# Moving the normalisations in a two-layer window attention: q's norm into the exponentials, the division by the sums to the values' output, and the first maxima ahead of two loads

## The chip, the core and the metric

The kernel runs on one core of one Trainium2 chip. The metric is the device time of one execution in microseconds (us). The core has five engines that follow their own instruction streams and meet at semaphores: PE (TensorE: matrix multiplications and the transposes made with them), DVE (VectorE), ACT (ScalarE), POOL (GpSimd) and SP (SyncE), which here only issues DMA transfers.

## What is computed

The input x is 4 x 1024 x 128 in float32. First comes a latent attention of 16 heads with 8 columns each, between two layer norms. Then come two layers, each made of a window attention of 8 heads with 64 columns and an MLP, and a last norm and residual. The change lies in the way that the first attention's rows of maxima are sent, and in the window attention, of which this is the core:

```python
q = l2norm(q) * qs                      # l2norm(t) = t / clip(|t|, 1e-12), per head
k = l2norm(k) * ksc
q, k = rotary_xpos(q, k)                # q * cos * scale + rotate_half(q) * sin * scale, k with / scale
bq = q.reshape(b, h, w, 64, d) * 8.0    # windows of 64 rows, QK_SCALE
sim = einsum('bhwid,bhwjd->bhwij', bq, bk)     # keys of this window and of the one before
attn = softmax(where(mask, -max, sim))
out = einsum('bhwij,bhwjd->bhwid', attn, bv)
x = x + out @ wo
```

The norm of q is one number for each row and head. It can be applied to q, or to q's scores. The sum of a row's exponentials is one number for each row and head as well. It can divide the probabilities, or the row of the output.

## The kernel before, in words

The kernel is five functions in a row, each a block in which all engines have a stream of their own: `project`, `attend` (the first attention), `mix`, then `window` and `mlp` twice, then `last_norm`.

In `project`, SP writes the bf16 parts of q and k of each chunk of 512 rows to DRAM (`send`, six transfers per chunk, 48 in all). `load_group` reads one group of four heads of one batch back from there, 576 KB for q (`a_qs`) and 576 KB for k (`a_ks`). SP's transfers go through one queue and are served in the order in which they are issued. Group 0 is loaded in `project`, between the sends of chunks 1 and 2; groups 1 to 3 are loaded at the start of `attend`.

In `attend`, DVE finds the rows' maxima of the scores, PE turns them (L463), ACT copies them to `a_nmT` (L513), and SP sends them to the last rows of `a_qs` (`send_maxima`, L391). PE's scores (L437) of a stage wait for these rows.

`window` works on 32 tiles of 128 rows each, in slots. In slot s, each engine does its steps of several tiles in a fixed order, written out in its `slot` function (`pipelined` for POOL): the projection, squares, sums of squares and the rotation of tile s, the normalising of tile s-1, the turns, scores, maxima and exponentials of tile s-2, the turned probabilities and the values of tile s-3, and the output of tile s-4. Even heads are half 0 and odd heads half 1, so maxima, bias and exponentials come in two halves. There is no planner: what stands first in a slot function is done first, and a wait holds all that stands behind it on its engine.

The names that are needed below, with their lines: `copy_raw` (ACT, L1010) takes q and k out of PSUM; `cosines` (DVE, L1137) and the four sine products (POOL, L1084) read them; POOL adds both (L1089, `w_rot`); ACT squares (L1015), DVE sums (L1128) and clips (`w_ssm`, L1132); POOL raises the sums to the power -1/2 (`norms`, L1095, `w_rn`); DVE multiplies (`normalise`, L1146, 1024 columns); PE turns q and k (L908); DVE and ACT copy them (L1152, L1155, L1026); PE makes scores (`scores`, L918, L925, L929); DVE finds maxima (L1161) and multiplies them by -8 (L1164); ACT exponentiates (L1033, eight instructions of 128 columns a tile, with the sums as a second output); DVE inverts the sums (L1174) and multiplies the probabilities (L1177, 1024 columns); PE turns them (L940), ACT and DVE copy them (L1040, L1169); PE makes the values (L955), already turned, heads on partitions; ACT copies them (L1045); PE multiplies by wo (L962, `out`); DVE adds to x (L1181).

## Time and profile before

| | us |
|---|---|
| time, median of 3 runs | 1649.61 (1644.88 to 1649.94) |
| time of the profiled execution | 1648.13 |
| its span, first to last instruction | 1646.4 |
| PE busy | 1320.4 (80%) |
| DVE busy | 1284.1 (78%) |
| ACT busy | 935.7 (57%) |
| POOL busy | 754.5 (46%) |

By stage, from the busy time in stretches of the profiled execution: `project` and the first maxima of `attend` up to 127.2 us, the rest of `attend` to 645.6 us, `mix` to 699 us, the first `window` to about 1065 us, its `mlp` to about 1160 us, the second `window` to 1527 us, and `mlp` and `last_norm` to the end. The two `window` stages take some 730 us of the 1646.

A busy share over the whole span says little here. The shares differ by stage, and an engine counts as busy while its instruction waits inside for a shared resource. So the stage has to be read from its slots: the instructions of one period, in order of time on each engine, with the idle time before them in brackets and what ended it.

### The profile page before, as it was taken

How to read it: one execution, taken by the hardware profiler on the slowest of the kernel's cores; microseconds unless marked ns; L12 is line 12 of the kernel's file. 1: busy time of each engine (PE TensorE's matmuls, PEld its weight loads, DVE VectorE, ACT ScalarE, POOL GpSimd, SP SyncE). 2: the span in 40 equal slices, each digit the busy share in tenths (PEclk: the TensorE clock that was granted, in tenths of full speed). 3: DMA queues.
4: the chain of work that ended last, by engine and by line, in shares of the span. 5: the costliest groups of instructions: out<-in, count | busy, mean ns of one | idle time of the engine just before them, and what ended most of it. 6: DMA issues, size and time to landing. Idle time of an engine off the chain costs nothing. (4 is left out here: it accounts for less than half of the span.)

```text
span 1646.4 us, 30935 instructions
## 1 busy us (share of the span) xinstructions
PE 1320.4 (80%) x11013; PEld 740.6 (45%) x11013; DVE 1284.1 (78%) x2674; ACT 935.7 (57%) x2589; POOL 754.5 (46%) x742
## 2 busy tenths in 40 slices
PE   4438999999999997368888888789588888887892
PEld 2213444444444433235555555555255555555551
DVE  6536777777777771659999999765599999998566
ACT  3203666766766766646666776532467666676230
POOL 1001122122122121488888888410688888885112
PEclk9755999999999998579999999989799999999796
DMA  4340011111111102011111111000111111110001
GB/s 105 112 114 8 27 37 33 54 41 34 50 45 33 34 4 74 21 44 32 33 34 33 29 30 32 14 1 1 47 29 31 33 33 34 33 26 21 1 1 51
DMA packets 44272, 59.59 MB, mean 36 GB/s; under 512 B 8130, under 2 KB 31948, under 8 KB 41804
## 3 DMA queue, kind: packets, MB, share of 16 engines
q1 hardware_dynamic: 43544, 57.47, 13.2%
q8 instruction: 89, 1.46, 0.4%
q14 instruction: 63, 0.52, 0.1%
q10 hardware_dynamic: 576, 0.15, 0.0%
HBM read 26.67 MB, written 8.39 MB: 21 GB/s over the span
## 5 line engine op out<-in xcount | busy, mean ns | idle before, releaser
L585 DVE TENSOR_REDUCE a_nm<-a_psM 128x1 f32<-128x512 f32 (+3 forms) x768 | 375.5, 551 | 137.2 <-PE a_psM L422 93.3
L507 ACT ACTIVATE a_prob<-a_psE 128x512 f32<-128x512 f32 (+3 forms) x768 | 322.9, 491 | 187.2 <-PE a_psE L437 186.2
L437 PE MATMUL a_psE<-a_qs,a_ks 84*128 84x512 bf16 (+3 forms) x768 | 251.7, 336 | 30.1 <-DMA a_qs<-a_nmT 26.0
L422 PE MATMUL a_psM<-a_ks,a_qs 72*128 72x512 bf16 (+3 forms) x768 | 255.6, 345 | 17.4 <-PEq L75 10.1
L1033 ACT ACTIVATE w_prob<-w_psS,w_bias 128x128 f32<-128x128 f32 x512 | 180.9, 366 | 145.2 <-DVE w_bias L1164 145.2
L541 POOL TENSOR_SCALAR_AFFINE_SELECT a_prob<-a_prob 128x512 f32<-128x512 f32 x128 | 81.1, 635 | 376.8 <-ACT a_prob L507 376.8
L1084 POOL TENSOR_TENSOR w_t<-w_raw,w_sin 128x256 f32<-128x256 f32 x256 | 212.5, 860 | 50.5 <-ACT w_raw L1010 50.5
L1095 POOL TENSOR_TENSOR w_rn<-w_ssm,mhalf 128x16 f32<-128x16 f32 x64 | 186.3, 2910 | 82.0 <-DVE w_ssm L1132 81.3
L1089 POOL TENSOR_TENSOR w_rot<-w_t 128x1024 f32<-128x1024 f32 x64 | 192.3, 3004 | 8.8 <-issue 0.4
L451 PE MATMUL a_psO<-a_prob,v_all 128*32 128x512 f32 (+3 forms) x1536 | 167.8, 504 | 0.0
L437 PEld LDWEIGHTS a_psE<-a_qs,a_ks 84*128 84x128 bf16 x768 | 74.3, 99 | 203.9 <-ACT a_prob L507 107.3
L896 PE MATMUL w_psQK<-w_wqkv,w_hT 128*128 128x512 f32 x256 | 133.1, 645 | 0.0
L1164 DVE TENSOR_SCALAR w_bias<-w_nmx 128x4 f32<-128x4 f32 x128 | 125.3, 979 | 4.4
L425 PE MATMUL a_psM<-mask_q,ident_b 128*128 128x128 bf16 x512 | 116.7, 229 | 0.0
L422 PEld LDWEIGHTS a_psM<-a_ks,a_qs 72*128 72x128 bf16 x768 | 76.8, 100 | 75.5 <-DVE a_nm L585 46.8
L918 PE MATMUL w_psS<-mask_w,ident_b 128*128 128x512 bf16 x128 | 39.5, 390 | 88.5 <-ACT w_qT L1026 76.7
L1033 ACT ACTIVATION_READ_ACCUMULATOR w_prob<-w_psS,w_bias 128x1 f32 x512 | 104.1, 203 | 0.0
L1137 DVE TENSOR_TENSOR w_t<-w_raw,w_cos 128x1024 f32<-128x1024 f32 x64 | 78.0, 1219 | 29.7 <-ACT w_raw L1010 24.9
L1146 DVE TENSOR_TENSOR w_rot<-w_rot,w_rn 128x1024 f32<-128x1024 f32 x64 | 94.2, 1471 | 2.5 <-POOL w_rn L1095 0.8
L1161 DVE TENSOR_REDUCE w_nmx<-w_psS 128x4 f32<-128x512 f32 x128 | 87.2, 681 | 3.4 <-PE w_psS L929 3.4
L1272 PE MATMUL f_psU<-f_hT,f_w 128*114 128x512 f32 (+1 forms) x192 | 88.5, 612 | 0.0
L955 PE MATMUL w_psO<-w_pT,w_vb 128*64 128x64 f32 x1024 | 58.3, 235 | 33.3 <-DVE w_pT L1169 17.3
(140 smaller groups left out, 2541.7 us busy)
## 6 DMA issues: line engine op xcount, KB each, us to landing
w_vb<-w_v SPq DMA_DIRECT2D x128, 128.0 KB, 2.3
a_qs<-q_parts SPq DMA_DIRECT2D x16, 576.0 KB
a_ks<-k_parts SPq DMA_DIRECT2D x16, 576.0 KB
w_xc<-xf_sb SPq DMA_DIRECT2D x64, 64.0 KB, 1.9
q_parts<-p_parts SPq DMA_DIRECT2D x24, 128.0 KB
k_parts<-p_parts SPq DMA_DIRECT2D x24, 128.0 KB
out_x<-l_y SPq DMA_DIRECT2D x8, 256.0 KB, 2.3
a_qs<-a_nmT SPq DMA_DIRECT2D x32, 48.0 KB
```

Of the source, the lines that this page charges most:

```text
L422: mm = pe.matmul(out, qs[0:ROWS, g, j, i * P:(i + 1) * P], ks[0:ROWS, g, j, 512 * kc:512 * kc + n], start=True, stop=not diag)
L425: mm = pe.matmul(out[:, n - P:n], sb["ident_b"], sb["mask_q"], start=False, stop=True)
L437: pe.matmul(psE[:, r % NRING, 0:w], ks[0:KROWS, g, j, kt * P:(kt + 1) * P], qs[0:KROWS, g, j, q0:q0 + w], start=True, stop=True).then_inc( ...
L451: mm = pe.matmul(psO[32 * j:32 * j + 32, qc, q0:512], v_flat[:, col + j * VA:col + j * VA + 32], prob[G % NPROB][:, j, 0:512 - q0], start= ...
L507: act.activation(prob[G % NPROB][:, j, 0:w], psE[:, r % NRING, 0:w], ACT.Exp, scale=SCALE0).then_inc(e_read, 1)
L585: dve.tensor_reduce(nm[:, s % 2, kc, i, j:j + 1], psM[:, r % NRING, 0:n], AX.X, ALU.max, negate=True).then_inc(m_read, 1)
L896: pe.matmul(psQK[:, w, :], hT[:, r % 2, 0:P], wqkv[:, bass.ds(layer * (3 * INNER) + w * INNER, INNER)], start=True, stop=True).then_inc(qk ...
L1033: i = act.activation(prob[:, p, w, c, :], psS[:, w, c * P:(c + 1) * P], ACT.Exp, bias=bias[:, p, n:n + 1], scale=QK_SCALE, accum_out=den[: ...
L1084: i = pool.tensor_tensor(out[:, w, :, half, :], src[:, w, :, 1 - half, :], tab, ALU.mult)
L1089: pool.tensor_tensor(rot[:, r % 2, :], t1[:, :], t2[:, :], ALU.add).then_inc(rot_done, 1)
L1095: pool.tensor_tensor(rn[:, p, :], ssm[:, p, :], sb["mhalf"][:, 0:16], ALU.pow).then_inc(rn_done, 1)
L1164: dve.tensor_scalar(bias[:, p, ns], nmx[:, p, ns], -QK_SCALE, None, ALU.mult).then_inc(bias_done, 1)
```

## The change

In `project`, `load_group` is also called for group 1, right behind group 0. In `attend`, SP sends the first two halves of the maxima before it issues the loads of groups 2 and 3.

In `window`:

- `normalise` multiplies only k (512 columns). q stays as it is, its factor 8 moves into the cosine and sine tables, and q's power goes to the exponentials as their scale, a column of `w_rn` for each head in place of a constant.
- The reduce of the maxima gives negated maxima, and the bias is now a tensor_tensor of the maxima and of q's powers in place of a tensor_scalar with a constant.
- `w_rn` has four buffers in place of two. `norms` has a lag of one slot and stands before `rotate`.
- The division by the sums: L1177 goes. The values now come out with rows on partitions; a new step `scale_o` on DVE multiplies them by the inverted sums out of PSUM into `w_on` (512 columns), and a new step `turn_o` on PE turns them back (four transposes).
- The order in a slot: `scale_o` of tile s-4 is DVE's first step. `turn_o` stands on PE between the projection of q and k and the turns of `w_rot`. `copy_oT` is ACT's first step, ahead of `copy_raw`. `residual` moves behind the first half of the maxima.

```diff
@@ project, SP @@
             load_group(sp, io, sb, 0, 0)
+            load_group(sp, io, sb, 0, 1)
@@ attend, SP @@
-            for g in range(1, NG):
+            send_maxima(0, 0)
+            send_maxima(0, 1)
+            for g in range(2, NG):
                 load_group(sp, io, sb, 0, g)
             for par in range(2):
                 sp.wait_ge(sb["parts_out"][par], 16 * 6 * (NCH // 2))
-            send_maxima(0, 0)
-            send_maxima(0, 1)
@@ window, PE @@
-                    at_least(pe, prob_done, base, t, 1)
+                    halves(pe, exp_done, t, 2)
...
-                for u, src in ((0, vb[r]), (1, v[r])):
-                    for i4 in range(4):
-                        h = 4 * b + i4
-                        c, w = h // 2, h % 2
-                        i = pe.matmul(psO[DH * w:DH * w + DH, c * P + WIN * u:c * P + WIN * (u + 1)], src[:, h * DH:(h + 1) * DH],
-                                      pT[:, b, i4, WIN * u:WIN * (u + 1)], start=True, stop=True, skip_group_check=True)
+                for i4 in range(4):
+                    h = 4 * b + i4
+                    for u, src in ((0, vb[r]), (1, v[r])):
+                        i = pe.matmul(psO[WIN * u:WIN * u + WIN, h * DH:(h + 1) * DH], pT[:, b, i4, WIN * u:WIN * (u + 1)],
+                                      src[:, h * DH:(h + 1) * DH], start=True, stop=True, skip_group_check=True)
                 i.then_inc(av_done, 1)
+
+            def turn_o(t, r):
+                at_least(pe, on_done, base, t, 1)
+                for c in range(4):
+                    i = pe.transpose(psO[:, c * P:(c + 1) * P], on[:, c * P:(c + 1) * P], sb["ident"])
+                i.then_inc(oT_done, 1)
@@ window, ACT @@
                     i = act.activation(prob[:, p, w, c, :], psS[:, w, c * P:(c + 1) * P], ACT.Exp,
-                                       bias=bias[:, p, n:n + 1], scale=QK_SCALE, accum_out=den[:, p, n:n + 1])
+                                       bias=bias[:, p, n:n + 1], scale=rn[:, r, 2 * c + w:2 * c + w + 1], accum_out=den[:, p, n:n + 1])
...
             def copy_oT(t, r):
-                halves(act, av_done, t, 2)
+                at_least(act, oT_done, base, t, 1)
@@ window, POOL @@
             def norms(t, r):
-                p = r % 2
                 at_least(pool, ssm_done, base, t, 1)
-                at_least(pool, unit_done, base, t, -1)
-                pool.tensor_tensor(rn[:, p, :], ssm[:, p, :], sb["mhalf"][:, 0:16], ALU.pow).then_inc(rn_done, 1)
+                at_least(pool, unit_done, base, t, -3)
+                halves(pool, exp_done, t, -6)
+                pool.tensor_tensor(rn[:, r, :], ssm[:, r % 2, :], sb["mhalf"][:, 0:16], ALU.pow).then_inc(rn_done, 1)
...
-            pipelined(pool, NT, 4, [(0, rotate), (0, norms)])
+            pipelined(pool, NT, 4, [(1, norms), (0, rotate)])
@@ window, DVE @@
-                both = rot[:, p, :].rearrange("p (h d) -> p h d", d=DH)
-                dve.tensor_tensor(both, both, rn[:, p, :].unsqueeze(2).broadcast_to((P, 16, DH)), ALU.mult).then_inc(unit_done, 1)
+                keys = rot[:, p, INNER:2 * INNER].rearrange("p (h d) -> p h d", d=DH)
+                dve.tensor_tensor(keys, keys, rn[:, r, HEADS:2 * HEADS].unsqueeze(2).broadcast_to((P, HEADS, DH)), ALU.mult).then_inc(unit_done, 1)
...
-                dve.tensor_scalar(bias[:, p, ns], nmx[:, p, ns], -QK_SCALE, None, ALU.mult).then_inc(bias_done, 1)
+                dve.tensor_tensor(bias[:, p, ns], nmx[:, p, ns], rn[:, r, w:HEADS:2], ALU.mult).then_inc(bias_done, 1)
...
                 dve.reciprocal(rden[:, p, :], den[:, p, :]).then_inc(rden_done, 1)
+
+            def scale_o(t, r):
+                p = r % 2
+                halves(dve, av_done, t, 2)
                 at_least(dve, rden_done, base, t, 1)
-                pr = prob[:, p, :, :, :].rearrange("p w c k -> p (w c) k")
-                dve.tensor_tensor(pr, pr, rden[:, p, :].unsqueeze(2).broadcast_to((P, HEADS, P)), ALU.mult).then_inc(prob_done, 1)
+                at_least(dve, oT_done, base, t, 0)
+                dve.tensor_tensor(on[:, :].rearrange("p (c w d) -> p w c d", w=2, d=DH), psO[:, :].rearrange("p (c w d) -> p w c d", w=2, d=DH),
+                                  rden[:, p, :].rearrange("p (w c) -> p w c", w=2).unsqueeze(3).broadcast_to((P, 2, 4, DH)), ALU.mult).then_inc(on_done, 1)
@@ window, DVE's slot @@
+                if runs(s - 4):
+                    scale_o(s - 4, r)
                 if runs(s - 2):
                     copy_kT(s - 2, r2)
                 if runs(s - 3):
                     divide(s - 3, r3)
-                if runs(s - 4):
-                    residual(s - 4, r)
                 if runs(s):
                     cosines(s, r)
                 if runs(s - 2):
                     maxima(s - 2, r2, 0)
+                if runs(s - 4):
+                    residual(s - 4, r)
```

DVE's instructions at the turn of a slot in the second window stage, before: from the end of one slot (the second maxima, bias and sums) to the first maxima of the next.

```order
1017 L1161 TENSOR_REDUCE w_nmx1<-w_psS_1 128x4
1018 L1164 TENSOR_SCALAR w_bias1<-w_nmx1 128x4
1019 L1128 TENSOR_REDUCE w_ss1<-w_sq1 128x16
1020 L1132 TENSOR_SCALAR w_ssm1<-w_ss1 128x16
1021 L1152 COPY w_kT1<-w_psT_1 128x4x128
1022 L1155 COPY w_kT1<-w_kT1 128x4x64
1023 L1174 RECIPROCAL w_rden1<-w_den1 128x8
1024 L1177 TENSOR_TENSOR w_prob1<-w_prob1,w_rden1 128x1024
1025 L1181 TENSOR_TENSOR xf_sb<-xf_sb,w_psO_1 128x128
1026 L1137 TENSOR_TENSOR w_t11<-w_raw1,w_cos1 128x1024
1027 L1161 TENSOR_REDUCE w_nmx1<-w_psS_1 128x4
```

The same place after the change:

```order
1016 L1171 TENSOR_REDUCE w_nmx1<-w_psS_1 128x4
1017 L1174 TENSOR_TENSOR w_bias1<-w_nmx1,w_rn1 128x4
1018 L1138 TENSOR_REDUCE w_ss1<-w_sq1 128x16
1019 L1142 TENSOR_SCALAR w_ssm1<-w_ss1 128x16
1020 L1191 TENSOR_TENSOR w_on1<-w_psO_1,w_rden1 128x2x4x64
1021 L1162 COPY w_kT1<-w_psT_1 128x4x128
1022 L1165 COPY w_kT1<-w_kT1 128x4x64
1023 L1184 RECIPROCAL w_rden1<-w_den1 128x8
1024 L1147 TENSOR_TENSOR w_t11<-w_raw1,w_cos1 128x1024
1025 L1171 TENSOR_REDUCE w_nmx1<-w_psS_1 128x4
1026 L1174 TENSOR_TENSOR w_bias1<-w_nmx1,w_rn1 128x4
1027 L1196 TENSOR_TENSOR xf_sb<-xf_sb,w_psO_1 128x128
```

The multiplication of `w_on` now stands right behind the sums of squares; the 1024 columns of `w_prob` are gone; the residual comes after the first bias.

PE's instructions in the first window stage from the projection of a slot's q and k to the scores, before:

```order
2345 L896 MATMUL w_psQK<-w_wqkv,w_hT 128x512 x2
2346 L908 MATMUL w_psT<-ident,w_rot 128x128 x8
2347 L962 MATMUL w_psO<-w_wo,w_oT 128x128 x4
2348 L900 MATMUL w_psV<-w_wqkv,w_hT 128x512
2349 L918 MATMUL w_psS<-mask_w,ident_b 128x512 x2
```

And after:

```order
2645 L899 MATMUL w_psQK<-w_wqkv,w_hT 128x512 x2
2646 L964 MATMUL w_psO<-ident,w_on 128x128 x4
2647 L911 MATMUL w_psT<-ident,w_rot 128x128 x8
2648 L970 MATMUL w_psO<-w_wo,w_oT 128x128 x4
2649 L903 MATMUL w_psV<-w_wqkv,w_hT 128x512
2650 L921 MATMUL w_psS<-mask_w,ident_b 128x512 x2
```

The four new transposes of `w_on` stand ahead of everything that leads to the scores.

SP's transfers at the start of `attend`, before (each pair of L68 and L69 is one group):

```order
60 L68 DMA a_qs<-q_parts 72x1x4096
61 L69 DMA a_ks<-k_parts 72x1x4096
62 L68 DMA a_qs<-q_parts 72x1x4096
63 L69 DMA a_ks<-k_parts 72x1x4096
64 L68 DMA a_qs<-q_parts 72x1x4096
65 L69 DMA a_ks<-k_parts 72x1x4096
66 L391 DMA a_qs<-a_nmT 12x4x512 x5
```

And after:

```order
62 L392 DMA a_qs<-a_nmT 12x4x512 x2
63 L68 DMA a_qs<-q_parts 72x1x4096
64 L69 DMA a_ks<-k_parts 72x1x4096
65 L68 DMA a_qs<-q_parts 72x1x4096
66 L69 DMA a_ks<-k_parts 72x1x4096
67 L392 DMA a_qs<-a_nmT 12x4x512 x3
```

Two of the maxima's transfers have moved ahead of the loads, and one group has left for `project`.

## Rows read from the trace of the kernel before

**Rows 1.** One line's instructions, the bias: duration ns min/median/max, first and last start us.

```profile
L1164 DVE TENSOR_SCALAR w_bias<-w_nmx x128: 170/662/1612, 725.3 to 1516.9; 128x4 f32<-128x4 f32 x128
```

**Rows 2.** Timeline, DVE, one slot: start us, length us, line, op, tiles.

```profile
836.17 1.43 DVE L1146 TENSOR_TENSOR w_rot<-w_rot,w_rn 128x1024 f32<-128x1024 f32 x1
837.52 0.68 DVE L1161 TENSOR_REDUCE w_nmx<-w_psS 128x4 f32<-128x512 f32 x1
838.23 1.60 DVE L1164 TENSOR_SCALAR w_bias<-w_nmx 128x4 f32<-128x4 f32 x1
```

**Rows 3.** Timeline, POOL, the same slot and the next power.

```profile
830.46 2.91 POOL L1095 TENSOR_TENSOR w_rn<-w_ssm,mhalf 128x16 f32<-128x16 f32 x1 [1.44 <-DVE w_ssm L1132]
833.33 3.18 POOL L1084 TENSOR_TENSOR w_t<-w_raw,w_sin 128x256 f32<-128x256 f32 x4
836.65 3.16 POOL L1089 TENSOR_TENSOR w_rot<-w_t 128x1024 f32<-128x1024 f32 x1
841.25 2.91 POOL L1095 TENSOR_TENSOR w_rn<-w_ssm,mhalf 128x16 f32<-128x16 f32 x1 [1.44 <-DVE w_ssm L1132]
```

**Rows 4.** Timeline, DVE, an early slot.

```profile
733.39 1.23 DVE L1177 TENSOR_TENSOR w_prob<-w_prob,w_rden 128x1024 f32<-128x1024 f32 x1
738.73 3.23 DVE L1146 TENSOR_TENSOR w_rot<-w_rot,w_rn 128x1024 f32<-128x1024 f32 x1
741.88 0.68 DVE L1161 TENSOR_REDUCE w_nmx<-w_psS 128x4 f32<-128x512 f32 x1
```

**Rows 5.** Timeline, POOL, the same early slot.

```profile
732.53 2.91 POOL L1095 TENSOR_TENSOR w_rn<-w_ssm,mhalf 128x16 f32<-128x16 f32 x1
738.52 2.35 POOL L1089 TENSOR_TENSOR w_rot<-w_t 128x1024 f32<-128x1024 f32 x1
744.17 2.91 POOL L1095 TENSOR_TENSOR w_rn<-w_ssm,mhalf 128x16 f32<-128x16 f32 x1 [3.30 <-DVE w_ssm L1132]
```

**Rows 6.** The sine products by tile: duration ns min/median/max, first and last start us.

```profile
L1084 POOL TENSOR_TENSOR w_t<-w_raw,w_sin x256: 708/726/1767, 705.2 to 1500.2; 128x256 f32<-128x256 f32 x128
```

**Rows 7.** Timeline, PE, one slot from the projection to the turned probabilities.

```profile
836.81 1.98 PE L896 MATMUL w_psQK<-w_wqkv,w_hT 128*128 128x512 f32 x4
838.63 1.04 PE L908 MATMUL w_psT<-ident,w_rot 128*128 128x128 f32 x8
839.50 1.06 PE L962 MATMUL w_psO<-w_wo,w_oT 128*128 128x128 f32 x8
840.40 1.02 PE L900 MATMUL w_psV<-w_wqkv,w_hT 128*128 128x512 f32 x2
842.83 0.61 PE L918 MATMUL w_psS<-mask_w,ident_b 128*128 128x512 bf16 x2 [1.41 <-ACT w_qT L1026]
844.40 0.77 PE L940 MATMUL w_psT<-ident,w_prob 128*128 128x128 f32 x5
```

**Rows 8.** Timeline, ACT, the copy of q and k in the next slot.

```profile
841.25 1.03 ACT L1010 ACTIVATE w_raw<-w_psQK 128x1024 f32<-128x1024 f32 x1
```

**Rows 9.** Timeline, SP and DVE, around the load of group 0 in project.

```profile
44.53 6.61 SPq L132 DMA_DIRECT2D k_parts<-p_parts  x1
...
59.11 0.69 DVE L229 CAST p_parts<-p_psQK 128x512 bf16<-128x512 f32 x1 [11.24 <-DMA k_parts<-p_parts]
```

**Rows 10.** Timeline, SP and PE, the loads of attend and the first two maxima.

```profile
89.49 0.81 SPq L68 DMA_DIRECT2D a_qs<-q_parts  x1
...
127.21 0.61 PE L437 MATMUL a_psE<-a_qs,a_ks 84*128 84x512 bf16 x1 [23.46 <-DMA a_qs<-a_nmT]
...
149.85 0.61 PE L437 MATMUL a_psE<-a_qs,a_ks 84*128 84x512 bf16 x1 [2.55 <-DMA a_qs<-a_nmT]
```

**Rows 11.** Groups by line, whole span: ACT with a tile as scale and bias; exponentials.

```profile
L738 ACT ACTIVATE m_an<-m_psA,m_shift,m_rstd 128x128 f32<-128x128 f32 x32 | 12.0, 458 | 6.2 <-DVE m_shift L768 6.2
...
L1033 ACT ACTIVATE w_prob<-w_psS,w_bias 128x128 f32<-128x128 f32 x512 | 180.9, 366 | 145.2 <-DVE w_bias L1164 145.2
```

**Rows 12.** Busy time in a stretch: PE, PEld, DVE, ACT, POOL, then PEclk, DMA share, GB/s.

```profile
750.00:1045.00 295.00, 240.68 (x2650) 159.86 (x2651) 288.83 (x412) 203.68 (x659) 253.70 (x165) 1.00 0.13 32
```

More of the change, by code:

```diff
@@ L832, in window @@
         oT = tile("w_oT", [P, 4, P])
+        on = tile("w_on", [P, INNER])
         psQK = ctx.enter_context(nc.psum_tensor(f"w_psQK_{layer}", [P, 2, 512], F32))
```

17 lines of the change are left out of this document (10 added, 7 removed).

## The prediction, written before the changed kernel had run

> **What bounds the kernel now.** I read the stages first, then one slot of `window` engine by engine, then the early slots, where the phases between the engines are different, and last the start of `attend`.
>
> In a steady slot POOL starts its power at 830.46 and the next one at 841.25: the period is 10.79 us [rows 3]. DVE has hardly a gap there, which looks like a full DVE. It isn't. The bias of 128x4 takes 1.60 us [rows 2], and 0.17 where nothing is in its way [rows 1]. It ends at 839.83, just when POOL's addition ends (836.65 + 3.16 = 839.81) [rows 2, 3]. So a DVE instruction can be held until a POOL instruction is over, and counts as busy meanwhile. The other direction shows as well: the addition takes 3.16 in that slot, where `normalise` (836.17 to 837.60) runs into it, and 2.35 where it comes first [rows 2, 3, 5].
>
> That gives the loop that sets the period: power to sines 2.87 (830.46 to 833.33), sines to addition 3.32 (833.33 to 836.65), addition 3.16, then the released bias, the sums and the clip until the next power, 1.44. Together 10.79 [rows 3]. PE waits 1.41 a slot for ACT's copy [rows 7]. What counts is not how much work DVE has, but what it still has to do between the end of POOL's addition and the sums.
>
> **The window stage, part by part.** I place the changed slot with the end of the clip as 0.
>
> *Ahead of the scores.* `scale_o` is DVE's next instruction. It reads 512 columns of PSUM; the reduce of 512 columns out of PSUM takes 0.68 [rows 2]. PE cannot go on to the turns before `turn_o` has it: four transposes, half of the eight that take 0.87 from start to start [rows 7], so 0.44, with 0.07 for the semaphore (estimate, from the 0.09 between clip and power) . Then the turns 0.87, `out` 0.90, the projection of v 1.02, and the scores 1.57 from start to start and some 0.1 until their end [rows 7]. So the scores end at 0.60 + 0.07 + 0.44 + 0.87 + 0.90 + 1.02 + 1.67 = 5.57. Before, PE did its turns without DVE's last results. On ACT the new scale from a tile makes an exponential dearer: 458 ns with scale and bias from tiles against 366 with a bias alone [rows 11], 8 x 0.09 = 0.7 a slot. ACT has waits of more than that, which hide it. ACT's copy of q and k now waits for `turn_o` and the copy of oT (at most 0.68, like the reduce of 512 columns) and takes 1.03 [rows 8]: it is over at 0.60 + 0.07 + 0.50 + 0.68 + 1.03, near 2.9.
>
> *POOL.* The order in the queue stays power, sines, addition: `norms` has moved from the end of a slot to the start of the next. The wider buffers remove no wait that the trace shows. The power starts at 0.09, the sines at 0.09 + 2.87 = 2.96, just when the copy is over. Before, `cosines` had started before the sines and cost them about 0.3 (3.18 for four of 0.726) [rows 3, 6]. Now it can't: it has the k copy behind the turns (which end at 2.1) and the reciprocal ahead of it and comes at about 3.2. It waits for the first sine product and then holds up the second. The longest sine product shows what that costs: 1767 - 726 = 1.04 [rows 6]. So the sines take 2.90 + 1.04 = 3.94, the addition starts after 0.14 more, at 7.04, and takes 2.35 [rows 5]: until 9.4.
>
> *The collision.* After the scores' end at 5.57, DVE does the maxima (0.71 to the next start [rows 2]), the bias (0.2; up to 0.7 if it meets the last sine product), residual, carry and a copy of 512 columns (0.2, 0.2 and, like the reduce, 0.7: some 1.15), and comes to `normalise` at 7.6 to 8.2. POOL's addition began at 7.04. Before, `normalise` was first by 0.48 (836.17 against 836.65) [rows 2, 3]. Where it comes second, the trace has it: the addition from 738.52 to 740.87, `normalise` from 738.73 with 3.23, where L1177 with as many columns takes 1.23, the next maxima at 741.88, 1.01 after the addition [rows 4, 5]. With 512 columns instead of 1024 it is 0.54 less (1.22 against 0.68): 0.47. From there to the next power it was 744.17 - 741.88 = 2.29 [rows 4, 5]: the second maxima, bias, sums, clip.
>
> *The sum for a slot.* 2.87 + 3.94 + 0.14 + 2.35 + 0.47 + 2.29 = 12.06 us, against 10.79: +1.27. What DVE gains is real (1.22 for the probabilities becomes 0.68, 1.22 of `normalise` becomes 0.68, the bias no longer waits 1.43), but it lies outside of the loop; inside it, maxima and bias (0.9) and half a `normalise` (0.47) now come after the addition. If DVE should be first after all, the bias, which reads two tiles, is held by the addition instead: 7.04 + 0.6 + 2.35 + 0.2 + 1.4 + 0.1 = 11.7, nearly the same.
>
> Here a rule of the Trainium skill bears on it (SBUF — State Buffer, Who interferes with whom): a VectorE instruction with two inputs in SBUF contends with a GpSimd instruction that reads SBUF, and whichever is first has the pair of ports for its whole length. By that rule, the bias as a tensor_tensor is no freer than as a tensor_scalar, and the trace agrees for `normalise` (3.23 against 1.23). For the power it does not: L1177 ran from 733.39 for 1.23, its usual length, inside a power from 732.53 to 735.44 [rows 4, 5]. By the letter of the rule the power too would hold such instructions; in the changed slot the SBUF to SBUF copy of kT would then wait some 0.1 (12.1 in place of 12.06), and the sum goes by the rows.
>
> *Over the stage.* A layer has 28 slots between the filling and the run-out: 2 x 28 x 1.27 = +71. In the run-out there are no sines; there `scale_o` and `turn_o` (1.1) come on the path and the multiplication of the probabilities (1.2) leaves it. I take +2 for a layer, bounds -3 and +6: together +4.
>
> The values keep count and size (16 products of 64 columns); they lie beside DVE's work. Cost nothing, bounds -0.1 and +0.1 a slot. q's factor in the tables costs nothing.
>
> **The start.** Before, the first maxima sit behind three groups: PE waits 23.46, and 2.55 for the next half, which has nothing ahead of it [rows 10]. With the loads behind them PE waits about 3: -20.4. The second half's send is no longer at the back either. Loads 2 and 3 now go out some 21 us after the first scores, and are needed later than they land; group 1 is there already. But group 1's load now sits in front of chunk 2's sends. Three groups took from 89.49 to nearly 127.21, so 12.4 each [rows 10]. DVE already waits 11.24 for these sends, and SP stood 6.61 in one of them [rows 9]. Nothing else covers it: +12.4, bounds +6.6 and +14. Sum of this part: -8 (bounds -14 and -2).
>
> **The sum.** The profiled execution took 1648.1 (span 1646.4), 0.1% under the median of 1649.6. 1648.1 + 71 + 4 - 8 = 1715. I forecast 1716.
>
> **Rivals.**
> 1. *The sines are not held up.* If `cosines` slips through beside them, the addition starts at 6.0 and ends at 8.4, and a slot is 11.0 (+0.23): 1648 + 13 + 4 - 8 = 1657. Against it: the 1.04, and that the bias would then come into the addition, which gives 12 again.
> 2. *Faster.* The wait is one of wide or older instructions, and `normalise` with 512 columns and the bias with 4 pass POOL. Then DVE and PE set the slot: 5.57 + 0.1 + 0.71 + 0.2 + 1.15 + 0.6 + 0.71 + 0.2 + 1.4 = 10.6, -0.15 a slot: 1648 - 8 + 4 - 8 = 1636. It decides from the point where `normalise` waits less than 1.5 us. For it: the trace has no two-input instruction as small as this. Against it: the tiny bias waited too, as a tensor_scalar.
> 3. *PE's clock.* PE now stands idle about 2.5 us in one piece, waiting for `scale_o`; the granted clock was at its upper level (2.4 GHz) throughout the steady slots [rows 12], with waits of 1.41 [rows 7]. If it falls to the lower one in many slots, the path from clip to scores and the copy of q and k come later, by at most 0.7 a slot: 1716 + 39 = 1755.
>
> **How the numbers follow.** Forecast (1700 to 1735) 0.62, rival 1 0.12, rival 2 0.16, rival 3 0.10. The range reaches from rival 1 to the lower part of rival 3, 1653 to 1748, and leaves out rival 2 and a few hundredths. A measurement of this kernel can tell about 0.3%, 5 us, from no change. Faster by more: rival 2 without its share near zero, 0.15. Within: 0.03. Slower: 0.82.
>
> **What would show it.** Right: a period of about 12 between powers; `normalise` near 1.5 to 2.4 us instead of 0.7, ending just after POOL's addition; POOL's addition at 2.35 instead of 3.16; one sine product in four at 1.7; PE idle 2 to 3 us until `w_on`; in `project` a wait of DVE near 23 instead of 11; the first scores' wait near 3. Wrong: `normalise` at 0.7 in the steady slots, a period under 11, or a DVE that waits for PE's scores longer than for POOL.

## The result: 4.8% slower, and the profile after

The changed kernel takes 1726.6 us (median of 4 runs, 1723.3 to 1730.6), the kernel before 1647.2 beside it: ratio 1.048, 95% interval 1.045 to 1.052. The forecast was 1716, so the direction and most of the size were right. The profiled execution has a span of 1721.6 against 1646.4: +75.2 us. Of the experiments below, e4 and e8 each had one execution in four that was far slower than the rest (6935 and 4332 us), and their ratios rest on the other three.

The sum of the changes along the program, read from the two timelines (layers 0 and 1 of the window stage; "power" is POOL's instruction that makes `w_rn`, one for each tile):

| stretch | change, us |
|---|---|
| start, up to the first power of `window` | -8.0 |
| powers 0 to 3 of a layer (filling) | -3.7 and -4.3 |
| powers 3 to 31 (28 slots) | +41.1 and +38.2 |
| last power to last residual (run-out) | +6.1 and +4.3 |
| the rest | +1.5 |

Most of it hangs on the steady slot, the time from one power to the next where all tiles take the same time. First DVE in one such slot of the changed kernel, as its timeline has it (start us, length us, engine, line, operation, tiles, shapes, and in brackets the idle time ahead and what ended it). All line numbers are some ten higher than before: L1191 is `scale_o`, L1147 the cosines, L1156 `normalise`, L1171 and L1174 maxima and bias, L1138 and L1142 sums and clip.

```profile
839.77 0.69 DVE L1191 TENSOR_TENSOR w_on<-w_psO,w_rden 128x512 f32<-128x512 f32 x1
842.09 0.69 DVE L1162 COPY w_kT<-w_psT 128x512 f32<-128x512 f32 x1 [1.63 <-PE w_psT L911]
...
843.01 1.64 DVE L1147 TENSOR_TENSOR w_t<-w_raw,w_cos 128x1024 f32<-128x1024 f32 x1
845.42 0.69 DVE L1171 TENSOR_REDUCE w_nmx<-w_psS 128x4 f32<-128x512 f32 x1 [0.77 <-PE w_psS L932]
846.14 0.48 DVE L1174 TENSOR_TENSOR w_bias<-w_nmx,w_rn 128x4 f32<-128x4 f32 x1
...
847.82 1.82 DVE L1156 TENSOR_TENSOR w_rot<-w_rot,w_rn 128x512 f32<-128x512 f32 x1
849.56 0.68 DVE L1171 TENSOR_REDUCE w_nmx<-w_psS 128x4 f32<-128x512 f32 x1
850.27 0.16 DVE L1174 TENSOR_TENSOR w_bias<-w_nmx,w_rn 128x4 f32<-128x4 f32 x1
850.36 1.21 DVE L1138 TENSOR_REDUCE w_ss<-w_sq 128x16 f32<-128x1024 f32 x1
851.60 0.17 DVE L1142 TENSOR_SCALAR w_ssm<-w_ss 128x16 f32<-128x16 f32 x1
```

POOL in the same slot: power L1105, sines L1094, addition L1099. It answers to [rows 3].

```profile
839.92 2.91 POOL L1105 TENSOR_TENSOR w_rn<-w_ssm,mhalf 128x16 f32<-128x16 f32 x1 [2.76 <-DVE w_ssm L1142]
842.81 3.80 POOL L1094 TENSOR_TENSOR w_t<-w_raw,w_sin 128x256 f32<-128x256 f32 x4
846.74 2.35 POOL L1099 TENSOR_TENSOR w_rot<-w_t 128x1024 f32<-128x1024 f32 x1
851.85 2.91 POOL L1105 TENSOR_TENSOR w_rn<-w_ssm,mhalf 128x16 f32<-128x16 f32 x1 [2.76 <-DVE w_ssm L1142]
```

The period is 851.85 - 839.92 = 11.93, where it was 10.79. Read against each other, the two lists are the whole loop. The sines take 3.80, because the cosines (1.64 instead of 1.23) run in the middle of them. The addition takes its plain 2.35 from 846.74 to 849.09. `normalise`, of half the size it had [rows 2], starts 1.08 after it and is held: 1.82 instead of 0.69, with the next maxima at 849.56. POOL's wait for the clip went from 1.44 [rows 3] to 2.76.

The groups by line, over the whole span (the last columns: busy us and mean ns of one, then idle time ahead and its releaser), show that this is how most slots look: `normalise` has a mean of 1627 ns, the addition of 2354, and PE waits 118.9 us in all ahead of `turn_o` (L964). An exponential takes 454 ns where it took 366 [rows 11], as the prediction had it.

```profile
L1043 ACT ACTIVATE w_prob<-w_psS,w_bias,w_rn 128x128 f32<-128x128 f32 x512 | 227.3, 454 | 99.7 <-DVE w_bias L1174 95.1
...
L1099 POOL TENSOR_TENSOR w_rot<-w_t 128x1024 f32<-128x1024 f32 x64 | 150.7, 2354 | 8.8 <-issue 0.4
L964 PE MATMUL w_psO<-ident,w_on 128*128 128x128 f32 x256 | 44.2, 298 | 118.9 <-DVE w_on L1191 118.9
...
L1147 DVE TENSOR_TENSOR w_t<-w_raw,w_cos 128x1024 f32<-128x1024 f32 x64 | 101.4, 1585 | 29.3 <-ACT w_raw L1020 24.4
...
L1156 DVE TENSOR_TENSOR w_rot<-w_rot,w_rn 128x512 f32<-128x512 f32 x64 | 104.2, 1627 | 2.8 <-POOL w_rn L1105 1.1
```

Not all slots take 11.93. Nine of the 56 take 12.2 to 13.8; together they hold 10.4 us more than the others. In the six longest ones (13.25 to 13.75) the granted clock of PE falls, in or right behind the idle piece ahead of `turn_o`. Two (12.42 and 12.43) follow such a slot and begin with the last of its slow stretch. The ninth, 12.23, has the clock at 1.00 throughout; in it POOL itself starts the addition 0.42 late, for no wait that the profile shows:

```profile
970.06 2.35 POOL L1099 TENSOR_TENSOR w_rot<-w_t 128x1024 f32<-128x1024 f32 x1 [0.42 <-issue]
```

One of the longest slots: busy time by stretch (us from the start; then the stretch's length, busy us and instructions of PE, PEld, DVE, ACT and POOL, the granted clock PEclk, DMA share, GB/s), and under it PE's timeline in the same place:

```profile
898.00:900.00 2.00, 0.19 (x1) 0.00 (x0) 1.94 (x4) 1.78 (x8) 0.40 (x1) 1.00 0.42 104
900.00:902.00 2.00, 1.79 (x9) 1.80 (x10) 0.15 (x1) 0.73 (x3) 2.00 (x1) 0.55 0.04 8
902.00:904.00 2.00, 2.00 (x13) 2.00 (x12) 0.94 (x2) 1.81 (x3) 1.57 (x3) 0.59 0.00 0
```

```profile
900.21 1.11 PE L964 MATMUL w_psO<-ident,w_on 128*128 128x128 f32 x4 [2.02 <-DVE w_on L1191]
901.11 1.92 PE L911 MATMUL w_psT<-ident,w_rot 128*128 128x128 f32 x8
```

The granted clock is at its lower level (1.2 GHz) for some 3 us; the eight turns take 1.92 instead of 1.04 [rows 7]. The scores come later, and the first bias, at 907.39, is then the one that falls into POOL's addition: 1.86 instead of 0.48.

At the start, DVE's wait in `project` and PE's first wait in `attend` are these (timelines):

```profile
70.78 0.69 DVE L230 CAST p_parts<-p_psQK 128x512 bf16<-128x512 f32 x1 [22.38 <-DMA k_parts<-p_parts]
```

```profile
118.54 0.61 PE L438 MATMUL a_psE<-a_qs,a_ks 84*128 84x512 bf16 x1 [3.28 <-DMA a_qs<-a_nmT]
```

The first wait grew from 11.24 [rows 9], the second fell from 23.46, and the first scores come 8.7 earlier than at 127.21 [rows 10].

### The profile page after: what moved, and what is told of

It reads as the page before. It is cut to its first block and busy times, and to the rows that moved or that the text cites. A ratio compares the mean times of both kernels' runs of the same rounds, so it can differ in the third digit from the quotient of the medians.

```text
span 1721.6 us, 31507 instructions
## 1 busy us (share of the span) xinstructions
PE 1371.3 (80%) x11269; PEld 788.2 (46%) x11269; DVE 1212.3 (70%) x2674; ACT 984.2 (57%) x2589; POOL 742.7 (43%) x742
## 5 line engine op out<-in xcount | busy, mean ns | idle before, releaser
L1043 ACT ACTIVATE w_prob<-w_psS,w_bias,w_rn 128x128 f32<-128x128 f32 x512 | 227.3, 454 | 99.7 <-DVE w_bias L1174 95.1
L1094 POOL TENSOR_TENSOR w_t<-w_raw,w_sin 128x256 f32<-128x256 f32 x256 | 241.8, 975 | 52.6 <-ACT w_raw L1020 52.6
L1105 POOL TENSOR_TENSOR w_rn<-w_ssm,mhalf 128x16 f32<-128x16 f32 x64 | 186.2, 2910 | 162.9 <-DVE w_ssm L1142 162.4
L1099 POOL TENSOR_TENSOR w_rot<-w_t 128x1024 f32<-128x1024 f32 x64 | 150.7, 2354 | 8.8 <-issue 0.4
L964 PE MATMUL w_psO<-ident,w_on 128*128 128x128 f32 x256 | 44.2, 298 | 118.9 <-DVE w_on L1191 118.9
L1171 DVE TENSOR_REDUCE w_nmx<-w_psS 128x4 f32<-128x512 f32 x128 | 87.7, 685 | 53.8 <-PE w_psS L932 53.8
L1147 DVE TENSOR_TENSOR w_t<-w_raw,w_cos 128x1024 f32<-128x1024 f32 x64 | 101.4, 1585 | 29.3 <-ACT w_raw L1020 24.4
L1162 DVE COPY w_kT<-w_psT 128x512 f32<-128x512 f32 x64 | 44.2, 691 | 105.3 <-PE w_psT L911 105.3
L957 PE MATMUL w_psO<-w_vb,w_pT 128*64 128x64 f32 x1024 | 85.1, 228 | 39.8 <-ACT w_pT L1050 29.6
L1156 DVE TENSOR_TENSOR w_rot<-w_rot,w_rn 128x512 f32<-128x512 f32 x64 | 104.2, 1627 | 2.8 <-POOL w_rn L1105 1.1
L964 PEld LDWEIGHTS w_psO<-ident,w_on 128*128 128x128 f32 x256 | 28.5, 146 | 165.9 <-DVE w_on L1191 165.3
L1043 ACT ACTIVATION_READ_ACCUMULATOR w_prob<-w_psS,w_bias,w_rn 128x1 f32 x512 | 102.3, 200 | 0.0
```

Of the source, the lines that this page charges most:

```text
L1043: i = act.activation(prob[:, p, w, c, :], psS[:, w, c * P:(c + 1) * P], ACT.Exp, bias=bias[:, p, n:n + 1], scale=rn[:, r, 2 * c + w:2 * c ...
L1094: i = pool.tensor_tensor(out[:, w, :, half, :], src[:, w, :, 1 - half, :], tab, ALU.mult)
L1099: pool.tensor_tensor(rot[:, r % 2, :], t1[:, :], t2[:, :], ALU.add).then_inc(rot_done, 1)
L1105: pool.tensor_tensor(rn[:, r, :], ssm[:, r % 2, :], sb["mhalf"][:, 0:16], ALU.pow).then_inc(rn_done, 1)
L1156: dve.tensor_tensor(keys, keys, rn[:, r, HEADS:2 * HEADS].unsqueeze(2).broadcast_to((P, HEADS, DH)), ALU.mult).then_inc(unit_done, 1)
```

## The experiments

"Slot" is the time between two powers on POOL in the steady part of `window`. Ratios are against the kernel before, with the 95% interval.

### The parts one by one

**e1_start_only.** The kernel before with the change's loads alone.

```diff
             load_group(sp, io, sb, 0, 0)
+            load_group(sp, io, sb, 0, 1)
...
-            for g in range(1, NG):
+            send_maxima(0, 0)
+            send_maxima(0, 1)
+            for g in range(2, NG):
                 load_group(sp, io, sb, 0, g)
```

> The kernel before with the change of the start alone (group 1 loaded in project, the first two sends of the maxima ahead of the loads of groups 2 and 3); the window stages as before. My theory: the first scores wait about 3 us instead of 23.5, DVE waits about 22.4 instead of 11.2 in project; together -8 us, so about 1639 to 1641 against 1647. Rival: the start gives nothing by itself, because the later loads then hold up a later stage: 1647.

Measured: 1639.4 us, ratio 0.996 (0.994 to 0.997), first scores' wait 3.29. The start gains the 8 us that the sum had.

**e2_one_group_ahead.** The same, but group 1 stays at the start of `attend`, ahead of the maxima, out of the way of `project`'s sends.

```diff
+            load_group(sp, io, sb, 0, 1)
+            send_maxima(0, 0)
+            send_maxima(0, 1)
-            for g in range(1, NG):
+            for g in range(2, NG):
                 load_group(sp, io, sb, 0, g)
```

> The kernel before, where SP issues group 1's load first in attend, then the two sends of the maxima, then the loads of groups 2 and 3; nothing is added to project. If a group takes 12.4 us in the queue, group 1 is through at about 102 us, before the maxima are ready at 104.4, so the first scores wait about 3 us and project is as short as before: -20 us, 1627. If the price of the load in project was not the queue but the transfers themselves (shared bandwidth), group 1 still holds up the maxima's send here, and the gain is under 12 us: over 1635.

Measured: 1628.2 us, ratio 0.989 (0.987 to 0.991). PE's timeline has the first scores another 12.5 earlier than in the changed kernel, with the same wait:

```profile
106.03 0.61 PE L438 MATMUL a_psE<-a_qs,a_ks 84*128 84x512 bf16 x1 [3.27 <-DMA a_qs<-a_nmT]
```

So group 1's load costs `project` about 12 us, as estimated from [rows 10], and the change gave away more than half of what sending the maxima earlier brings (8 us in place of 19). The loads' place in the queue is what counts: group 1's load ahead of the maxima in `attend` did not hold them up.

**e3_fold_only.** The kernel before with q's norm in the exponentials and the power a slot later; the division stays on the probabilities.

```diff
-bias=bias[:, p, n:n + 1], scale=QK_SCALE,
+bias=bias[:, p, n:n + 1], scale=rn[:, r, 2 * c + w:2 * c + w + 1],
...
-pipelined(pool, NT, 4, [(0, rotate), (0, norms)])
+pipelined(pool, NT, 4, [(1, norms), (0, rotate)])
...
-dve.tensor_tensor(both, both, rn[:, p, :].unsqueeze(2)...
+dve.tensor_tensor(keys, keys, rn[:, r, HEADS:2 * HEADS].unsqueeze(2)...
...
-dve.tensor_scalar(bias[:, p, ns], nmx[:, p, ns], -QK_SCALE, None, ALU.mult)
+dve.tensor_tensor(bias[:, p, ns], nmx[:, p, ns], rn[:, r, w:HEADS:2], ALU.mult)
```

> The kernel before with the fold of q's norm alone: k normalised alone, q's powers as the exponentials' scale and in the bias, four buffers of powers, powers a slot later in the code; probabilities divided as before, start as before. My theory (the loop through POOL's addition): normalise is still first at the port, and is 0.54 us shorter, so the addition starts and ends earlier by that and the slot is 10.25 instead of 10.79: 56 x -0.54 = -30 us, about 1617. Rival, the fold is what costs (two tiles in the bias, a scale from a tile in 512 exponentials): slower than 1647, up to 1700.

Measured: 1617.7 us, ratio 0.982 (0.981 to 0.984), slot 10.26. DVE's and POOL's timelines in a slot:

```profile
839.65 0.90 DVE L1146 TENSOR_TENSOR w_rot<-w_rot,w_rn 128x512 f32<-128x512 f32 x1
840.47 0.68 DVE L1161 TENSOR_REDUCE w_nmx<-w_psS 128x4 f32<-128x512 f32 x1
841.18 1.60 DVE L1164 TENSOR_TENSOR w_bias<-w_nmx,w_rn 128x4 f32<-128x4 f32 x1
```

```profile
840.14 2.62 POOL L1089 TENSOR_TENSOR w_rot<-w_t 128x1024 f32<-128x1024 f32 x1
844.20 2.91 POOL L1095 TENSOR_TENSOR w_rn<-w_ssm,mhalf 128x16 f32<-128x16 f32 x1 [1.44 <-DVE w_ssm L1132]
```

Here `normalise` is still ahead of the addition and costs it 0.27 instead of 0.81 [rows 3, 5]: the fold alone is a gain. The bias of four elements, now with two input tiles, ends at 842.78, when the addition does (842.76): the small size frees nothing. That takes away rival 2's ground for the bias.

**e4_division_only.** The changed kernel with the fold and the new loads undone (the inverse of the two diffs above).

> The kernel before with the division at the values' output alone (scale_o, turn_o, the new order in the slots); q and k normalised as before, bias as before, start as before. My theory: the collision of normalise with POOL's addition comes with the new order, and normalise is 0.54 us longer than in the changed kernel: slots of about 12.45 instead of 11.93, 1727 + 8 (start) + 30 = about 1765. Rival, the fold is what costs: this one is then near or under 1647.

Measured: 1796.1 us, ratio 1.090 (1.088 to 1.092). The quiet slots take 12.46, as expected. But 24 of the 56 take 13.3 to 14.6 and hold some 37 us in all, which the expectation did not have. In each of them the granted clock falls near an idle piece of PE ahead of `turn_o` (2.55, in the first of each layer 3.2 and 3.3); in eight others the same 2.55 leaves it up. PE's timeline and the busy time by stretch of one:

```profile
863.66 1.12 PE L963 MATMUL w_psO<-ident,w_on 128*128 128x128 f32 x4 [2.55 <-DVE w_on L1190]
```

```profile
864.00:866.00 2.00, 2.00 (x11) 2.00 (x10) 0.00 (x0) 1.19 (x2) 1.97 (x1) 0.50 0.00 0
```

The parts don't add up. The fold alone gains 30 us, the division alone costs 149, the start gains 8: together a loss of 111, where the whole change loses 79. Next to the fold the division costs less, above all since PE's idle piece is 2.02 instead of 2.55 and its clock falls in 6 slots instead of 24 (10 against 37 us).

### What sets the slot of the changed kernel

**e12_after_no_normalise.** `normalise` is left out, so k stays as it is. Its semaphore waits go too (not shown): PE's turns wait for POOL's addition instead, and the maxima for the power. All else is in place.

```diff
-                if runs(s - 1):
-                    normalise(s - 1, (r - 1) % 4)
                 if runs(s - 2):
                     maxima(s - 2, r2, 1)
```

> Changed kernel in which k is not normalised (`normalise` left out, all else in place). Theory (the chain behind POOL's addition sets the slot): DVE then has the second maxima done when the addition ends, its bias alone is held until then (849.09 in the slot from 839.92), and sums, clip and power follow in 1.44, as in the kernel before: 2.9 + 3.8 + 0.13 + 2.35 + 1.44 = 10.6 instead of 11.93, a gain of 1.3 from work of 0.68: 1727 - 56 x 1.3 - 10 (the slots at the fallen clock) = 1644, between 1638 and 1662. Rival (DVE's own work, not the addition, sets the slot): a gain of 0.7 a slot, 1688; and none, 1727, if PE does.

Measured: 1640.0 us, ratio 0.995 (0.993 to 0.997), slot 10.61. The work taken out is 0.69 us a slot, the gain 1.32. DVE's and POOL's timelines:

```profile
845.68 0.68 DVE L1171 TENSOR_REDUCE w_nmx<-w_psS 128x4 f32<-128x512 f32 x1
846.39 0.69 DVE L1174 TENSOR_TENSOR w_bias<-w_nmx,w_rn 128x4 f32<-128x4 f32 x1
847.00 1.21 DVE L1137 TENSOR_REDUCE w_ss<-w_sq 128x16 f32<-128x1024 f32 x1
```

```profile
844.71 2.35 POOL L1099 TENSOR_TENSOR w_rot<-w_t 128x1024 f32<-128x1024 f32 x1
848.50 2.91 POOL L1104 TENSOR_TENSOR w_rn<-w_ssm,mhalf 128x16 f32<-128x16 f32 x1 [1.44 <-DVE w_ssm L1141]
```

The second bias is now the one that meets the addition and ends with it (847.08 and 847.06), and the 1.44 of the kernel before is back. PE waited for `w_on` here too (0.69), and the slot fell all the same. That the gain is nearly twice the work is the most direct evidence for the loop. The granted clock stays up in all steady slots.

**e8_v_first.** The projection of v ahead of `turn_o` on PE.

```diff
+                if runs(s):
+                    project_v(s, r)
                 if runs(s - 4):
                     turn_o(s - 4, r)
...
-                if runs(s):
-                    project_v(s, r)
```

> Changed kernel with the projection of v put ahead of `turn_o` in PE's slot, so that it fills part of the 2.0 us in which PE waits for `w_on`; the scores then end 0.86 earlier. If the slots of 12.4 to 13.8 us come from PE's granted clock, which falls after such idle pieces: they go away, some 10 us, and the steady slot stays at 11.93, since its loop runs over POOL and DVE: 1716, between 1712 and 1719. If the long slots have another cause: 1727. If PE's way to the scores sets the slot: 0.8 a slot less, 1680.

Measured: 1714.2 us, ratio 1.040 (1.038 to 1.042). The steady slot stays at 11.93, though the scores no longer have v's projection ahead of them: PE's way is not what sets it. The total is as expected, its make-up only in part. Of the long slots two are left (12.22 and 13.30, which hold 1.7 us instead of 10.4), and the last two slots of each layer fell from 11.9 to 11.06 (3.5 us). The first has POOL's own 0.42 ahead of the addition again, with the clock up. Right behind it, in the second, the clock falls, the only time before the last slot of a layer. But PE's idle piece ahead of `turn_o` only shrank from 2.02 to 1.84, since its values come earlier as well; in the slot where the clock fell it was 2.08. Fewer falls of the clock after shorter idle pieces fits the theory; how the chip decides it, these runs don't show.

**e5_after_sums_first.** DVE's sums and clip ahead of `normalise`.

```diff
+                if runs(s):
+                    sums(s, r)
                 if runs(s - 1):
                     normalise(s - 1, (r - 1) % 4)
                 if runs(s - 2):
                     maxima(s - 2, r2, 1)
-                if runs(s):
-                    sums(s, r)
```

> Changed kernel with one thing moved: in DVE's slot the sums and the clip of the tile come ahead of `normalise` and the second maxima. Theory (the loop that sets the slot is power, sines, addition on POOL, and then half a `normalise`, the second maxima, a bias, the sums and the clip, 0.47 + 2.29, which DVE can only do after the addition): the sums now lie beside the addition, the clip ends with it, and the power follows at once. What then sets the slot is DVE's own round with PE, from `scale_o` to the scores (839.77 to 845.3) and through maxima, bias, residual, copy, sums, clip, `normalise`, maxima, bias until 850.8: 11.0 us instead of 11.93. 56 x 0.93 = 52: 1727 - 52 = 1675, between 1665 and 1690. Rival (the loss is the way through PE alone: `w_on` is waited for, and clip to scores is what got long): the order of what stands behind the scores does not matter, 11.9 a slot, 1727.

Measured: 1674.8 us, ratio 1.016 (1.014 to 1.018). The loss is not in PE's way alone; 52 of the 79 us go by an order on DVE (the long slots' 10.4 among them). The slot is 11.24, though, and not 11.0, and in POOL's timeline it has another form:

```profile
845.02 3.29 POOL L1105 TENSOR_TENSOR w_rn<-w_ssm,mhalf 128x16 f32<-128x16 f32 x1 [0.23 <-DVE w_ssm L1142]
849.72 3.83 POOL L1094 TENSOR_TENSOR w_t<-w_raw,w_sin 128x256 f32<-128x256 f32 x4 [1.41 <-ACT w_raw L1020]
853.67 2.35 POOL L1099 TENSOR_TENSOR w_rot<-w_t 128x1024 f32<-128x1024 f32 x1
```

The power follows the addition at 0.23, and then the sines wait 1.41 for ACT's copy of q and k. ACT does that copy behind the second half's exponentials, and these wait for the second bias, which DVE writes after the addition and `normalise`. A new loop, POOL to DVE to ACT to POOL, took the old one's place. That the total came out at 1675 is in part luck: 0.24 a slot (13 us) was missing against the expected slot, and the long slots, 10.4 us, are gone here.

### The two gains together, and the order of DVE on top

**e6_fold_start.** e2_one_group_ahead and e3_fold_only in one.

> Kernel before with q's norm folded into the exponentials (and the power a slot later), and with the first maxima sent one group earlier: the two parts that gained, without the division at the values' output. If they add up: 1618 - 19 = 1598 to 1599. Slot 10.26, first scores' wait near 3.3 at 106 us.

Measured: 1597.8 us, ratio 0.971 (0.968 to 0.973), slot 10.26. The two add up within 1 us, as edits of different stages do. It beats both kernels.

**e7_fold_start_sums.** The same, with the diff of e5_after_sums_first.

> The kernel of e6_fold_start with the sums and the clip ahead of `normalise` and the second maxima in DVE's slot. By the theory of the POOL loop the 1.3 or so of sums and clip no longer follow the addition, and the slot falls from 10.26 to 9.3 to 9.6, where DVE itself is full: 1598 - 56 x 0.8 = 1553, between 1540 and 1575. By the rival (PE's way sets the slot) it stays at 1598.

Measured: 1642.9 us, ratio 0.997 (0.995 to 0.998): 45 slower than e6, where 45 faster was expected. Neither theory had that; the slot is 10.94. POOL's timeline:

```profile
841.74 3.29 POOL L1096 TENSOR_TENSOR w_rn<-w_ssm,mhalf 128x16 f32<-128x16 f32 x1
845.95 4.13 POOL L1085 TENSOR_TENSOR w_t<-w_raw,w_sin 128x256 f32<-128x256 f32 x4 [0.92 <-ACT w_raw L1011]
850.22 2.36 POOL L1090 TENSOR_TENSOR w_rot<-w_t 128x1024 f32<-128x1024 f32 x1
```

The power follows the addition at once, and the slot is longer: the sines wait for ACT's copy, and at 4.13 they have more of DVE beside them. The copy stands behind the exponentials of the second half, and these behind the second bias. In e6 that bias ends with the addition (842.08 and 842.06) and the copy is over 1.5 us before the sines start. Here `normalise` and the second maxima come between the addition's end (841.64) and the bias (842.89), so the copy starts 3.21 after the addition instead of 1.81. The new order made that second loop longer while it shortened the first; the theory had the first one right and didn't price the second.

**e9_fold_start_maxima_together.** e6 with both maxima right behind the scores, and `normalise` last, which is to take the second bias out of that loop.

```diff
                 if runs(s - 2):
                     maxima(s - 2, r2, 0)
+                if runs(s - 2):
+                    maxima(s - 2, r2, 1)
...
-                if runs(s - 1):
-                    normalise(s - 1, (r - 1) % 4)
-                if runs(s - 2):
-                    maxima(s - 2, r2, 1)
                 if runs(s):
                     sums(s, r)
+                if runs(s - 1):
+                    normalise(s - 1, (r - 1) % 4)
```

> Kernel of e6_fold_start with another order in DVE's slot: both maxima and biases right after the scores, then carry, the copy of pT, the sums and clip, and `normalise` last. In e7_fold_start_sums (slot 10.95) the sines wait 0.92 for the copy of q and k on ACT, which stands behind the second half's exponentials, and these behind the second bias, which DVE writes only after the addition. Theory (that this round, addition to `normalise`, maxima, bias, four exponentials, copy, sines, took the place of the old one): with both biases ahead of the addition the copy is there in time, POOL is never idle for long, and the slot is power 3.0 to 3.3, sines 4.0, addition 2.36 and the gaps: 9.4 to 9.9, so 1598 - 56 x 0.6 = 1564, between 1548 and 1580. Rival (DVE has no room, its order is all the same): 10.3 to 11 a slot, 1598 to 1643.

Measured: 1786.4 us, ratio 1.085 (1.083 to 1.086), slot 13.7. A plain miss of 220 us. The first four steady slots of layer 0 take 10.47 to 10.56. Then one takes 14.03, and all others, in layer 1 too, 13.1 to 14.2. Busy time by stretch before and after the turn; then PE's timeline at the turn, and in a later slot:

```profile
751.00:756.00 5.00, 5.00 (x57) 3.48 (x56) 3.46 (x7) 3.98 (x10) 5.00 (x3) 1.00 0.28 66
...
762.00:764.00 2.00, 2.00 (x7) 1.09 (x6) 0.00 (x0) 1.33 (x5) 2.00 (x1) 0.50 0.43 107
```

```profile
759.61 0.45 PE L956 MATMUL w_psO<-w_pT,w_vb 128*64 128x64 f32 x8 [1.64 <-DVE w_pT L1170]
...
856.08 0.45 PE L956 MATMUL w_psO<-w_pT,w_vb 128*64 128x64 f32 x8 [3.16 <-DVE w_pT L1170]
856.36 0.50 PE L956 MATMUL w_psO<-w_pT,w_v 128*64 128x64 f32 x8
856.79 3.53 PE L897 MATMUL w_psQK<-w_wqkv,w_hT 128*128 128x512 f32 x4
```

PE waits for the copy of pT (1.64 in the early slots, 3.16 in the later ones), the granted clock is 0.50 to 0.57 in the stretches of the projections behind it, these take 3.53 instead of 1.98, DVE gets its turned k late, its second bias falls into the addition (853.41, 1.65), the copy of pT behind it comes late, and PE waits again.

**e10_after_maxima_together.** The changed kernel with the same order.

> Changed kernel with the same order in DVE's slot: both maxima after the scores, then residual, carry, copy of pT, sums and clip, `normalise` last. In e5_after_sums_first (slot 11.24) the sines wait 1.41 for the copy of q and k, behind the second half's exponentials and the copy of oT. By the same theory that wait goes, and what sets the slot is the way `scale_o`, `turn_o`, turns, `out`, v, scores (5.6), two maxima and biases (1.7), residual, carry, copy of pT (1.1), sums and clip (1.3), `normalise` (0.7): 10.3 to 10.5 us, so 1675 - 56 x 0.85 = 1627, between 1612 and 1642. That would make the division at the output a small loss or none against before (1648), and show that its price in the changed kernel is DVE's order behind it. Rival (the division costs its time whatever stands behind it): 11.2 to 11.9, 1675 to 1727.

Measured: 1808.2 us, ratio 1.098 (1.096 to 1.100), slot 13.65, with the same picture: second bias 1.84, PE idle 3.0 ahead of the values (once 3.3), projections 2.93. It is a miss of 181 us, and only in part for the same reason. The first steady slot of each layer has the clock up until its last 2 us and takes 12.46 and 12.45 all the same: the second bias comes 0.52 after the start of POOL's addition and is held there. POOL's and DVE's timelines of the first of them:

```profile
739.53 2.34 POOL L1099 TENSOR_TENSOR w_rot<-w_t 128x1024 f32<-128x1024 f32 x1
```

```profile
740.05 1.84 DVE L1174 TENSOR_TENSOR w_bias<-w_nmx,w_rn 128x4 f32<-128x4 f32 x1
```

So, as far as these two slots show, 2.0 of the 3.2 us that a slot is over its forecast come from a bias that this order was to take out of the collision and did not, and the fallen clock adds the last 1.2. Whether the division could be made cheap by another order stays open.

**e11_maxima_together_pe_filled.** e9 with the second half of the values behind the next projections, so that PE has work where it waited.

```diff
                     project_qk(s, r, 0)
                     project_qk(s, r, 1)
+                if runs(s - 4):
+                    values(s - 4, r, 1)
...
                     turn_x(s + 2, (r + 2) % 4)
-                if runs(s - 3):
-                    values(s - 3, r3, 1)
```

> Kernel of e9_fold_start_maxima_together with one thing moved on PE: the second four heads' values of a tile come behind the next tile's projections of q and k, so that these fill the 3.16 us in which PE waits for the copy of pT. In e9 the first slots took 10.55 and all later ones 13.7, with granted clock 0.51 to 0.57 in the projections behind that wait (3.55 us instead of 1.98). Theory (the idle piece makes the clock fall, the slow projections make the next idle piece, and so the slow slot holds itself): without the idle piece the clock stays at its upper level and the slot is 10.5, power 3.29, sines 4.65, addition 2.36 and 0.25: 1598 + 56 x 0.25 = 1612, between 1598 and 1635. Rival (the bias that is held 1.65 by the addition, and DVE behind it, make the 13.7): it stays over 1740.

Measured: 1609.5 us, ratio 0.978 (0.975 to 0.981), slot 10.23. POOL's and PE's timelines:

```profile
843.48 3.29 POOL L1096 TENSOR_TENSOR w_rn<-w_ssm,mhalf 128x16 f32<-128x16 f32 x1 [0.16 <-DVE w_ssm L1133]
846.74 4.34 POOL L1085 TENSOR_TENSOR w_t<-w_raw,w_sin 128x256 f32<-128x256 f32 x4
851.21 2.35 POOL L1090 TENSOR_TENSOR w_rot<-w_t 128x1024 f32<-128x1024 f32 x1
```

```profile
840.19 1.88 PE L897 MATMUL w_psQK<-w_wqkv,w_hT 128*128 128x512 f32 x4
...
844.06 1.09 PE L909 MATMUL w_psT<-ident,w_rot 128*128 128x128 f32 x8 [1.37 <-DVE w_rot L1147]
```

177 us come back because the values of four heads now stand behind the two projections. PE's idle pieces are 1.37 in nearly all slots, the granted clock over the steady part of layer 0 (720 to 1000 us) is 1.00, where e9 had 0.89 over its own (720 to 1080), and POOL has hardly a gap. One slot of layer 1 takes 12.62: its second bias falls into the addition (1.84), with the clock up, and the next slot takes 10.24 again. So a held bias alone does not keep itself going; in e9 the fallen clock kept it going. The kernel gains only 0.03 a slot on e6, all the same: POOL is now full, but dearer, since power (3.29) and sines (4.34 instead of 3.19) have DVE's two-input instructions beside them. In all it is 12 us slower than e6, which lies outside of the steady slots: the last two slots of a layer take 10.2 instead of 9.1, one takes the 12.62, and the stretches before, between and after the slots take some 8 us more; the filling gives back 3.

## Why the prediction was right, point by point

- **The loop.** Forecast: power, sines, addition, half a `normalise`, then maxima, bias, sums and clip; 12.06. Measured: 2.89 + 3.80 + 0.13 + 2.35 + 0.47 + 2.29 = 11.93. Five of the six terms came within 0.02. PE's wait for `w_on`, put at about 2.5, was 2.02. The sines were put at 3.94 and took 3.80: the cosines hold them for 0.90 and not for the 1.04 of the longest product [rows 6]. e12 and e5 confirm that the part behind the addition is on the loop, and e8 that PE's way is not.
- **Why it got slower.** Against e3 (10.26), where the division stays on the probabilities, the slot has +0.61 in the sines (3.80 against 3.19), -0.28 in the addition (2.35 against 2.63), and +1.32 from the addition's end to the power (2.76 against 1.44). Both losses are matters of which engine is first. `scale_o` and the wait for the turned k put the cosines into the middle of the sines, and `normalise` behind the start of the addition instead of before it.
- **The stage.** +71 was forecast for the slots, +79.3 measured. 56 x 1.145 = 64.1 are the steady slots. 10.4 are the nine long slots; all but 0.3 of it are slots with a fallen clock, which the forecast left to rival 3. The other 4.8 are the last two slots of a layer, which took 9.6 before and now take 11.9; the forecast counted them like the others.
- **Filling and run-out.** For the run-out +4 was forecast and +10.4 measured: the term was under-sized, and the bound of +6 a layer is what layer 0 took. The filling, which the sum left out, gained 8.0. The two errors nearly cancel, by luck.
- **The start.** -8 forecast, -8.0 measured. Of the two terms, the wait for the first maxima fell by 20.2 (-20.4 forecast), and `project`'s wait grew by 11.1 (+12.4 forecast). e2 shows that the second was avoidable.
- **Rival 3** had the right mechanism and was given as an alternative to the forecast, where it came on top of it. Its price of at most 0.7 a slot was too low: a slot in which the clock falls is up to 1.8 longer in the changed kernel, up to 2.1 in e4, and 3.2 in e9, since the slow PE work also moves a DVE instruction into POOL's addition. It was sized by the matmuls alone. In the changed kernel few slots fell, so the total stayed near the forecast: the steady slots came out 7 us under it, the clock 10 over, and that these two nearly cancel is luck as well.
- **Rival 1 and rival 2** fell: the sines are held (3.80), and `normalise` with 512 columns (1.82 instead of 0.69) and the two-input bias with 4 (1.60 in e3) do wait.
- **The shared port.** `normalise` is held by the addition (1.82), and in e3 the bias is held to its end. The clip, a tensor_scalar of 128x16, is held too where it meets the addition (0.94 instead of 0.17 in e7). In e6 the multiplication of the probabilities starts 0.87 after a power and takes its plain 1.23, and the power its plain 2.91. The Trainium skill (SBUF — State Buffer, Who interferes with whom) says that the first of a two-input VectorE instruction and a GpSimd instruction that reads SBUF keeps the ports for its whole length. For sines and addition the trace agrees; for a power that comes first it does not.

## What to carry to other kernels

Where two engines can hold each other, the slot is set by who comes first, not by how much work either has: draw the slot with the start of each two-input DVE instruction against each POOL instruction, before and after an edit, and price what stands between POOL's end and its next start. When a loop is cut, look for the next one and for what the edit adds to it (e7), and for the engine that gets an idle piece from it: in e9 a PE that came to stand still for some 3.2 us in every slot lost its upper clock in each of them, and the slot with it, and e11 got it back. Test a large edit in its parts: here the fold and, with one load fewer in `project`, the earlier maxima gave 3% (e6), and the division hid it.
